# Later gathers for slices 1 to 3, and the last dense layer in four column parts side by side

## The chip, the cores and the metric

One core of a Trainium2 chip runs the whole program. The metric is the device time of one execution in microseconds (us), the median of several runs. Engines: PE (matmul; PEld is its weight load), DVE (vector), ACT (scalar), POOL (GpSimd, which issues the gathers) and SP (which issues plain DMAs).

## The reference

A recommendation tower. For each of 1024 samples, 32 ids pick rows of 64 floats from 32 tables; every pair of the 32 rows is combined through its own 64 x 64 matrix, and the 496 results with 16 dense inputs pass through three layers.

```python
e = jnp.stack([tbl_0[ids[:, 0]], ..., tbl_31[ids[:, 31]]], axis=1)      # 1024 x 32 x 64
z = jnp.einsum('bpe,fpe,bpf->bp', e[:, iu], kernel, e[:, ju])           # 1024 x 496
h = jnp.concatenate([z, dense_ctx], axis=1)                             # 1024 x 512
h = jnp.maximum(h @ W_top1 + b_top1, 0.0)                               # 512
h = jnp.maximum(h @ W_top2 + b_top2, 0.0)                               # 256
y = h @ W_top3                                                          # 1
```

## The kernel before

The batch is cut into 8 slices of 128 samples (t = 0 to 7; TILES in the code), and two slices make a quarter of 256 samples, on which the dense layers run. The 32 fields of a slice are 16 packs of two. Each field is one gather: an indirect DMA that POOL issues (line 356), 128 rows of 64 floats into the ring `raw`, 256 gathers in all, in the order of slices and fields. When both gathers of a pack have landed (`gathered`), PE transposes it (line 611, into `prep_ps`) and ACT copies it to `xt` (line 394, a "fill").

The pair work of a slice is 32 units (NU), of three kinds: F (PE line 570, DVE multiply line 476), C (PE line 600, DVE line 498) and B (PE line 587, DVE lines 517 and 533). A unit's matmuls go to one of three slots of `t_ps`; PE counts `t_done` up by one when they are done, DVE waits for it and multiplies, and PE may use the slot again after that (`prod_done`). The F products are summed on PE in rounds of four units (line 642, into `z_ps`): matmuls with 32 columns of weights, 256 columns each, that rotate over four blocks of 32 result rows. The C and B products are summed along their 64 elements by ACT (line 418, one instruction a cell) and DVE (line 504), those of the last slice by POOL (line 374).

The matrices (`kmat`, 8.29 MB) are loaded by SP in the order in which the first slice needs them. In slices 0 to 3 the units are sorted by the last pack that they need, so that a slice can begin before all its fields are there.

PE, ACT and DVE each follow one list written ahead of time, SCHEDULE: units in order, with fills, rounds of sums and pieces of the dense layers inserted at set unit numbers (`fills_of`, GROUPS_AT, PAIRS_AT). The fills of slices 1 to 3 stand at these places, counted from the slice's own first unit: slice 1 at -5, -2, 1, 4, 8, 13, 17; slice 2 at -6, -2, 1, 4, 8, 12, 20; slice 3 (four packs each) at -6, -3, 4, 10. Slice 4's stand at -19, -12, -4, 4, and slices 5 to 7 have theirs at -20, -12, -4, 4.

POOL has no list of its own. `gather_after(t, field)` is the number of finished units (`t_done`) for which a gather waits: none for the first 16 gathers of slice 0, then (field - 12) // 2, and for later slices (t - 1) * 32 + field, so that a slice's gathers run one unit apart during the slice before it. Gathers whose number is reached already follow one another without a wait. The ring `raw` holds three slices, and from slice 3 on the first gather of each group of eight also waits until the group that was there is used up.

The dense layers of the first three quarters are pieces of PE's list: each result goes to `prep_ps` and is copied by ACT. The last quarter's stand at the end in `t_ps`. The last layer (line 710) takes two matmuls of 256 columns, `w3` one column of weights; ACT copies the row of 256 results (line 441) and issues the store (line 446).

The semaphores named in the text: `t_done` (PE to DVE and POOL), `prod_done` (DVE to PE and ACT), `prep_done` (PE to ACT) and `prep_copied` (ACT to PE).

Of the kernel before, what the change touches and what calls it, by code (L numbers as in the profile page):

```python
# [5 lines left out]
H1, H2 = 512, 256  # L6
P = 128
# [3 lines left out]
QB = 2 * P  # L11
# [24 lines left out]


def gather_after(t, field):


    return (t - 1) * NU + field if t else (field - 12) // 2 if field >= 16 else 0

# [147 lines left out]
TURN_LAG, PIECE_LAG, PIECE_STEP = 16, 24, 8  # L190
SUMS_LAG = 5
LAYER1, LAYER2 = H1 // P, H2 // P
PIECES = LAYER1 + LAYER2 + 1
# [74 lines left out]
def build(nc, ids, tables, kmat, dense, w1, b1, w2, b2, w3, sel, ident, y):  # L268
# [3 lines left out]
    with ctx:  # L272
# [10 lines left out]
        w2_sb = sb("w2_sb", [P, H1 // P, H2])  # L283
        w3_sb = sb("w3_sb", [P, H2 // P])
        b1_sb = sb("b1_sb", [P, H1 // P])
# [10 lines left out]
        h2 = sb("h2", [P, H2 // P, QB])  # L296
        y_sb = sb("y_sb", [1, 2, QB])

# [79 lines left out]
        def _(act):  # L378
# [42 lines left out]
            def copy_layer(q, piece):  # L421
# [9 lines left out]
                if piece < LAYER1:  # L431
                    nc.scalar.activation(h1[:, piece, :], source, ACT.Relu,
                                         bias=b1_sb[:, piece:piece + 1]).then_inc(copied, 1)
                elif piece < LAYER1 + LAYER2:
                    m = piece - LAYER1
                    nc.scalar.activation(h2[:, m, :], source, ACT.Relu, bias=b2_sb[:, m:m + 1]).then_inc(copied, 1)
                else:
                    if q >= 2:

                        act.wait_ge(y_stored[q % 2], 16 * (q // 2))  # L440
                    nc.scalar.activation(y_sb[:, q % 2, :], source[0:1, :], ACT.Copy).then_inc(copied, 1)
                    if q < QUARTERS - 1:
                        act.wait_ge(prep_copied, PREP_COUNT["piece", q, piece])
                    else:
                        act.wait_ge(layer_copied, PIECES)
                    act.dma_start(y[:, q * QB:(q + 1) * QB], y_sb[:, q % 2, :]).then_inc(y_stored[q % 2], 16)

# [101 lines left out]
        def _(pe):  # L549
# [146 lines left out]
            def later_layer(q, piece, out, copied, done):  # L696
# [9 lines left out]
                else:  # L706
                    for t in range(LAYER2):
                        if copied:
                            pe.wait_ge(copied, LAYER1 + t + 1)
                        last = nc.tensor.matmul(out[0:1, :], w3_sb[:, t:t + 1], h2[:, t, :],  # L710
                                                start=(t == 0), stop=(t == LAYER2 - 1))
                last.then_inc(done, 1)
# [87 lines left out]
```

## Time and profile before

| | us |
|---|---|
| median of 3 runs | 483.64 |
| lowest and highest of them | 479.96 and 483.74 |
| the profiled execution, its own time | 483.11 |
| its span, first to last instruction | 481.3 |
| PE busy | 411.4 (85%) |
| DVE busy | 342.4 (71%) |
| ACT busy | 325.4 (68%) |
| POOL busy | 268.3 (56%) |
| mean granted clock of PE | 0.957 of full speed |

The span is what the trace shows; the execution's own time has 1.8 us around it. Each fp32 matmul of the program stands in the trace as two weight loads and two matmuls. "x16" after an instruction is the number of records that were merged into the row. What stands behind "<-" in brackets is what ended the idle time before the instruction; "issue" means that the profile shows nothing that it waited for, "remote" and "another core or an unknown queue" that the signal has no visible sender.

### The profile page before, as it was taken

How to read it: one execution, taken by the hardware profiler on the slowest of the kernel's cores; microseconds unless marked ns; L12 is line 12 of the kernel's file. 1: busy time of each engine (PE TensorE's matmuls, PEld its weight loads, DVE VectorE, ACT ScalarE, POOL GpSimd, SP SyncE). 2: the span in 40 equal slices, each digit the busy share in tenths (PEclk: the TensorE clock that was granted, in tenths of full speed). 3: DMA queues.
4: the chain of work that ended last, by engine and by line, in shares of the span. 5: the costliest groups of instructions: out<-in, count | busy, mean ns of one | idle time of the engine just before them, and what ended most of it. 6: DMA issues, size and time to landing. Idle time of an engine off the chain costs nothing.

```text
span 481.3 us, 12047 instructions
## 1 busy us (share of the span) xinstructions
PE 411.4 (85%) x4144; PEld 280.4 (58%) x4144; DVE 342.4 (71%) x428; ACT 325.4 (68%) x2456; POOL 268.3 (56%) x308
## 2 busy tenths in 40 slices
PE   0554358888898988999999999999999999999997
PEld 0332245655556555767666666666666566666875
DVE  0044158889798878788778887888888788877820
ACT  1244215078967887689857897878786978988512
POOL 5757735566556555555545555556555555577400
PEclk9976568999998999999999999999999999999999
DMA  8751101015111111111111111111111111000000
GB/s 278 268 215 27 26 14 24 18 24 155 21 23 21 20 24 21 21 22 22 23 19 20 23 23 21 20 24 21 20 24 23 22 21 20 16 1 3 1 2 0
DMA packets 12756, 19.17 MB, mean 40 GB/s; under 512 B 6036, under 2 KB 6296, under 8 KB 12568
## 3 DMA queue, kind: packets, MB, share of 16 engines
q0 software_dynamic: 8192, 8.40, 9.4%
q1 hardware_dynamic: 2592, 8.29, 4.8%
q10 hardware_dynamic: 1912, 1.71, 1.2%
q8 instruction: 33, 0.54, 0.5%
q14 instruction: 27, 0.22, 0.1%
HBM read 18.39 MB, written 0.00 MB: 38 GB/s over the span
## 4 chain that ended last, share of the span: by engine, by line
PE 74%; DVE 12%; issue 9%; another core or an unknown queue 2%; DMA 2%; POOL 1%; ACT 1%; DVEq 0%
PE t_ps L570 25%; PE z_ps L642 14%; PE t_ps L600 12%; PE t_ps L587 9%; DVE prod L476 6%; PE prep_ps L657 5%; PE prep_ps L611 3%; DVE prod_a L498 2%; PE prep_ps L704 2%; DVE prod_a L517 2%; PE t_ps L657 2%; DVE zb L504 1%; DMA raw<-tbl,ids_sb 1%; POOL raw L356 1%
## 5 line engine op out<-in xcount | busy, mean ns | idle before, releaser
L356 POOL DMA_INDIRECT raw<-tbl,ids_sb x256 | 242.3, 946 | 172.5 <-issue 48.0
L418 ACT ACTIVATE prod_a<-prod_a 128x64 f32<-128x64 f32 x1184 | 283.9, 243 | 69.0 <-DVE prod_a L533 33.5
L418 ACT ACTIVATION_READ_ACCUMULATOR prod_a<-prod_a 128x1 f32 x1184 | 223.9, 189 | 7.5 <-issue 7.5
L476 DVE TENSOR_TENSOR prod<-t_ps,xt 128x1024 f32<-128x1024 f32 x128 | 155.7, 1220 | 63.6 <-PE t_ps L570 25.5
L570 PEld LDWEIGHTS t_ps<-xt,k_sb 64*128 64x128 f32 x2048 | 136.5, 193 | 55.3 <-issue 31.7
L570 PE MATMUL t_ps<-xt,k_sb 64*128 64x128 f32 x2048 | 151.7, 286 | 19.3 <-issue 10.1
L498 DVE TENSOR_TENSOR prod_a<-t_ps,raw 128x1024 f32<-128x1024 f32 x64 | 78.0, 1219 | 23.6 <-PE t_ps L600 14.7
L600 PE MATMUL t_ps<-k_sb,xt 64*128 64x512 f32 x256 | 74.7, 654 | 19.3 <-issue 14.1
L517 DVE TENSOR_TENSOR prod_a<-t_ps,raw 128x768 f32<-128x768 f32 (+2 forms) x96 | 62.9, 683 | 31.1 <-PE t_ps L587 24.0
L642 PE MATMUL z_ps<-prod,sel_sb 128*32 128x256 f32 x1024 | 71.7, 390 | 4.0 <-issue 3.7
L587 PE MATMUL t_ps<-k_sb,xt 64*128 64x384 f32 (+5 forms) x448 | 66.0, 402 | 3.5 <-issue 1.8
L642 PEld LDWEIGHTS z_ps<-prod,sel_sb 128*32 128x32 f32 x1024 | 33.9, 111 | 39.0 <-issue 22.6
L587 PEld LDWEIGHTS t_ps<-k_sb,xt 64*128 64x128 f32 x448 | 43.0, 191 | 21.9 <-issue 9.6
L394 ACT ACTIVATE xt<-prep_ps 128x512 f32<-128x512 f32 (+2 forms) x47 | 21.0, 446 | 42.6 <-PE prep_ps L611 31.0
L504 DVE TENSOR_REDUCE zb<-prod_a 128x8 f32<-128x512 f32 x76 | 49.7, 676 | 0.0
L611 PE MATMUL prep_ps<-ident_sb,raw 128*128 128x128 f32 x128 | 26.4, 305 | 20.8 <-DMA raw<-tbl,ids_sb 15.1
L600 PEld LDWEIGHTS t_ps<-k_sb,xt 64*128 64x128 f32 x256 | 21.0, 191 | 32.5 <-issue 23.7
L611 PEld LDWEIGHTS prep_ps<-ident_sb,raw 128*128 128x128 f32 x128 | 14.3, 144 | 38.0 <-issue 25.8
L374 POOL TENSOR_TENSOR prod_a<-prod_a 128x512 f32<-128x512 f32 (+4 forms) x40 | 24.3, 607 | 9.7 <-DVE prod_a L498 7.2
L533 DVE TENSOR_TENSOR prod_a<-t_ps,raw 128x128 f32<-128x128 f32 x64 | 18.0, 281 | 0.0
L657 PE MATMUL prep_ps<-zbt,w_sb 128*128 128x256 f32 x48 | 13.6, 405 | 0.0
L657 PE MATMUL prep_ps<-zt,w_sb 128*128 128x256 f32 x48 | 12.3, 379 | 0.0
(30 smaller groups left out, 91.1 us busy)
## 6 DMA issues: line engine op xcount, KB each, us to landing
raw<-tbl,ids_sb POOLq DMA_INDIRECT x256
k_sb<-kmat SPq DMA_DIRECT2D x4, 768.0 KB
k_sb<-kmat SPq DMA_DIRECT2D x4, 512.0 KB
k_sb<-kmat SPq DMA_DIRECT2D x4, 448.0 KB, 4.6
k_sb<-kmat SPq DMA_DIRECT2D x4, 256.0 KB
w_sb<-w ACTq DMA_DIRECT2D x1, 1024.0 KB
w_sb<-w ACTq DMA_DIRECT2D x1, 512.0 KB
ids_sb<-ids SPq DMA_DIRECT2D x1, 128.0 KB, 2.4
```

What stands on the lines that cost most here:

```text
L356: nc.gpsimd.indirect_dma_start(raw[:, n % RING, begin:begin + EMBED], None, tables[2 * k + f], bass.IndirectOffsetOnAxis(ap=ids_sb[:, t, 2 ...
L418: last = nc.scalar.activation(product, product, ACT.Copy, accum_out=zb[:, unit[1], at:at + 1])
L476: nc.vector.tensor_tensor(prod[:, own].rearrange("p n (m b) -> p (n m) b", b=P), t_ps[:, slot].rearrange("p n (m b) -> p (n m) b", b=P), x ...
L498: nc.vector.tensor_tensor(out, product, rows.unsqueeze(1).broadcast_to([P, 2, W]), ALU.mult).then_inc(prod_done, 1)
L504: nc.vector.tensor_reduce(zb[:, unit[1], begin + n * cells:begin + (n + 1) * cells], prod_a[:, NTH[unit] % ARING, n, 0:cells * EMBED].rear ...
L517: return nc.vector.tensor_tensor(out[:, :, cols], product[:, :, cols], rows[:, fields * EMBED:(fields + cells) * EMBED].unsqueeze(1).broad ...
L570: last = nc.tensor.matmul(t_ps[:, slot, n, i * P:(i + 1) * P], k_sb[rows, cols], xt[rows, x, :], start=True, stop=True)
L587: last = nc.tensor.matmul(product[:, n, cell * EMBED:(cell + cells) * EMBED], xt[rows, slot_of(t, GROUP * g + field // 2), :], k_sb[rows, ...
L600: last = nc.tensor.matmul(product[:, n, :], xt[rows, slot_of(t, k), :], k_sb[rows, COL["C", k, j]], start=True, stop=True)
L611: last = nc.tensor.transpose(prep_ps[:, n * P:(n + 1) * P], raw[:, group % RING, at * P:(at + 1) * P], ident_sb[:])
L642: last = nc.tensor.matmul(z_ps[32 * group:32 * group + 32, 0:ZBLOCKS * P], sel_sb[:, 30 - 2 * pos:62 - 2 * pos], prod[:, (t * NF + u) % FR ...
L657: return nc.tensor.matmul(out, w1_sb[:, part, m * P:(m + 1) * P], z, start=(part == ZBLOCKS), stop=(part == ZBLOCKS - 1 and half != 0))
```

## The change

Two edits. First, the gathers of slices 1, 2 and 3 wait for 10, 8 and 4 more finished units than before; those of slice 0 and of slices 4 to 7 keep their numbers. Second, the last dense layer is cut into four parts of 64 columns. `w3` gets 32 columns of weights, of which only the first is not zero; part n writes result rows 32n to 32n+31 and columns 0 to 63, so the four parts lie side by side on different rows. ACT copies 128 x 64 instead of 1 x 256, and the store takes every 32nd row, four rows of 256 B. The host reads `y` as 16 rows of 64 and reshapes it.

```diff
+GATHER_LATER = {1: 10, 2: 8, 3: 4}
 def gather_after(t, field):
-    return (t - 1) * NU + field if t else (field - 12) // 2 if field >= 16 else 0
+    return (t - 1) * NU + field + GATHER_LATER.get(t, 0) if t else (field - 12) // 2 if field >= 16 else 0
...
+YPARTS = 4
+YROWS, YCOLS = P // YPARTS, QB // YPARTS
...
-        w3_sb = sb("w3_sb", [P, H2 // P])
+        w3_sb = sb("w3_sb", [P, H2 // P, YROWS])
-        y_sb = sb("y_sb", [1, 2, QB])
+        y_sb = sb("y_sb", [P, 2, YCOLS])
...
-                    nc.scalar.activation(y_sb[:, q % 2, :], source[0:1, :], ACT.Copy).then_inc(copied, 1)
+                    nc.scalar.activation(y_sb[:, q % 2, :], source[:, 0:YCOLS], ACT.Copy).then_inc(copied, 1)
-                    act.dma_start(y[:, q * QB:(q + 1) * QB], y_sb[:, q % 2, :]).then_inc(y_stored[q % 2], 16)
+                    act.dma_start(y[q * YPARTS:(q + 1) * YPARTS, :], y_sb[0:P:YROWS, q % 2, :]).then_inc(y_stored[q % 2], 16)
...
-                        last = nc.tensor.matmul(out[0:1, :], w3_sb[:, t:t + 1], h2[:, t, :],
-                                                start=(t == 0), stop=(t == LAYER2 - 1))
+                        for part in range(YPARTS):
+                            last = nc.tensor.matmul(out[part * YROWS:(part + 1) * YROWS, 0:YCOLS], w3_sb[:, t, :],
+                                                    h2[:, t, part * YCOLS:(part + 1) * YCOLS],
+                                                    start=(t == 0), stop=(t == LAYER2 - 1))
...
+    w3_rows = np.zeros((P, H2 // P, YROWS), w1.dtype)
+    w3_rows[:, :, 0] = np.asarray(W_top3).reshape(-1, P).T
```

On POOL the gathers keep their order; what a row shows beside them is on which semaphores they wait. The program's start on POOL before, gathers of slice 0 (32), then of later slices:

```order
L356 DMA raw<-tbl,ids_sb 128x64 [waits ids_in]
L356 DMA raw<-tbl,ids_sb 128x64 x15
L356 DMA raw<-tbl,ids_sb 128x64 [waits t_done] x16
L356 DMA raw<-tbl,ids_sb 128x64
L356 DMA raw<-tbl,ids_sb 128x64 [waits t_done] x63
L356 DMA raw<-tbl,ids_sb 128x64 [waits t_done,prod_done]
L356 DMA raw<-tbl,ids_sb 128x64 [waits t_done] x7
```

The same place on POOL now:

```order
L362 DMA raw<-tbl,ids_sb 128x64 [waits ids_in]
L362 DMA raw<-tbl,ids_sb 128x64 x15
L362 DMA raw<-tbl,ids_sb 128x64 [waits t_done] x80
L362 DMA raw<-tbl,ids_sb 128x64 [waits t_done,prod_done]
L362 DMA raw<-tbl,ids_sb 128x64 [waits t_done] x7
```

Slice 1's first gather had no wait and has one now; the numbers waited for, which the rows don't show, are 10, 8 or 4 higher for the 96 gathers of slices 1 to 3.

On PE the rows are the same but for the last layer's. The program's end on PE before (`h` is h1 or h2):

```order
L657 MATMUL t_ps<-zt,w_sb 128x128 x2
L642 MATMUL z_ps<-prod,sel_sb 32x256 x16
L657 MATMUL t_ps<-zt,w_sb 128x128 x8
L704 MATMUL t_ps<-h,w_sb 128x256 x8
L710 MATMUL t_ps<-h,w_sb 1x256 x2
```

The program's end on PE now:

```order
L663 MATMUL t_ps<-zt,w_sb 128x128 x2
L648 MATMUL z_ps<-prod,sel_sb 32x256 x16
L663 MATMUL t_ps<-zt,w_sb 128x128 x8
L710 MATMUL t_ps<-h,w_sb 128x256 x8
L717 MATMUL t_ps<-h,w_sb 32x64 x8
```

Two matmuls of 1 x 256 have become eight of 32 x 64; nothing around them moved. The same holds for the three earlier places of that layer.

## Rows read from the trace of the kernel before

**Rows 1.** The page: the span, and its 40 equal slices of PE.

```profile
span 481.3 us, 12047 instructions
...
PE   0554358888898988999999999999999999999997
...
PEclk9976568999998999999999999999999999999999
```

**Rows 2.** Chain that ended last, 0 to 66 us: start us, us, what.

```profile
21.31 4.65 another core or an unknown queue
...
30.07 4.70 another core or an unknown queue
...
44.61 11.02 issue
...
60.13 4.97 issue
```

**Rows 3.** Timeline of POOL, 0 to 95 us: start, us, instruction, idle before.

```profile
3.38 1.09 POOL L356 DMA_INDIRECT raw<-tbl,ids_sb  x1 [2.93 <-DMA ids_sb<-ids]
...
22.30 0.94 POOL L356 DMA_INDIRECT raw<-tbl,ids_sb  x1 [0.30 <-issue]
26.18 0.95 POOL L356 DMA_INDIRECT raw<-tbl,ids_sb  x1 [2.94 <-remote]
...
32.44 0.95 POOL L356 DMA_INDIRECT raw<-tbl,ids_sb  x1 [0.30 <-issue]
35.03 0.95 POOL L356 DMA_INDIRECT raw<-tbl,ids_sb  x1 [1.64 <-remote]
...
46.28 0.95 POOL L356 DMA_INDIRECT raw<-tbl,ids_sb  x1 [0.30 <-issue]
...
60.04 0.94 POOL L356 DMA_INDIRECT raw<-tbl,ids_sb  x1 [0.30 <-issue]
64.93 0.95 POOL L356 DMA_INDIRECT raw<-tbl,ids_sb  x1 [3.94 <-remote]
```

**Rows 4.** Timeline of PE, 0 to 95 us.

```profile
10.53 0.45 PE L611 MATMUL prep_ps<-ident_sb,raw 128*128 128x128 f32 x1 [10.53 <-DMA raw<-tbl,ids_sb]
...
42.75 1.86 PE L570 MATMUL t_ps<-xt,k_sb 64*128 64x128 f32 x16
55.64 2.08 PE L600 MATMUL t_ps<-k_sb,xt 64*128 64x512 f32 x4 [11.02 <-issue]
...
58.05 2.08 PE L570 MATMUL t_ps<-xt,k_sb 64*128 64x128 f32 x16
65.11 2.08 PE L570 MATMUL t_ps<-xt,k_sb 64*128 64x128 f32 x16 [4.97 <-issue]
...
89.59 1.16 PE L570 MATMUL t_ps<-xt,k_sb 64*128 64x128 f32 x16 [0.59 <-DVE prod L476]
90.69 1.93 PE L642 MATMUL z_ps<-prod,sel_sb 128*32 128x256 f32 x32
```

**Rows 5.** Timeline of DVE, 0 to 95 us.

```profile
58.38 1.22 DVE L476 TENSOR_TENSOR prod<-t_ps,xt 128x1024 f32<-128x1024 f32 x1 [14.70 <-PE t_ps L600]
```

**Rows 6.** Timeline of ACT, 0 to 75 us.

```profile
19.79 0.24 ACT L418 ACTIVATE prod_a<-prod_a 128x64 f32<-128x64 f32 x1
...
49.44 0.26 ACT L394 ACTIVATE xt<-prep_ps 128x128 f32<-128x128 f32 x1
...
64.73 0.28 ACT L394 ACTIVATE xt<-prep_ps 128x128 f32<-128x128 f32 x1 [0.57 <-remote]
```

**Rows 7.** Busy time by stretch: stretch, us, PE, PEld, DVE, ACT, POOL, clock, DMA.

```profile
65.10:90.70 25.60, 22.76 (x246) 16.09 (x246) 21.64 (x27) 7.95 (x61) 14.13 (x16) 0.87 0.11 20
```

**Rows 8.** Timeline of PE, its weight loads and ACT, the last layer.

```profile
478.04 1.23 PE L710 MATMUL t_ps<-h,w_sb 128*1 128x256 f32 x4
...
478.67 0.09 PEld L710 LDWEIGHTS t_ps<-h,w_sb 128*1 128x1 f32 x2 [0.55 <-ACT h L436]
479.31 0.37 ACT L441 ACTIVATE y_sb<-t_ps 1x256 f32<-1x256 f32 x1 [0.68 <-PE t_ps L710]
```

More of the change, by code:

```diff
@@ L785 @@
         "b2": np.ascontiguousarray(np.asarray(b_top2).reshape(-1, P).T),
-        "w3": np.ascontiguousarray(np.asarray(W_top3).reshape(-1, P).T),
+        "w3": w3_rows,
         "sel": sel,
@@ L795 @@
            for n, a in arrays.items()}
-    y = nc.dram_tensor("y", (1, BATCH), mybir.dt.float32, kind="ExternalOutput").ap()
+    y = nc.dram_tensor("y", (QUARTERS * YPARTS, YCOLS), mybir.dt.float32, kind="ExternalOutput").ap()
     build(nc, tables=[aps.pop(f"tbl_{f}") for f in range(FIELDS)], y=y, **aps)
```

## The prediction

> **What bounds the kernel now.** I read the page first: the span of 481.3 us and the slices [rows 1]. The span is cut into 40 slices of 12 us: PE is 80% or more busy from the seventh on, but only 30 to 59% from the second to the sixth, and the granted clock sinks to 0.5 in the fifth. So something is wrong between about 20 and 70 us, in the first slice of the batch; after it PE works at a steady pace to the end, and what is saved there should move the whole rest forward. Next the chain that ended last [rows 2]: in the first 66 us four pieces stand out, two of "another core or an unknown queue" (4.65 and 4.70 us) and two of "issue" (11.02 and 4.97 us), 25.3 us in which the engine on the path waits for nothing that the profile can name. Gathers explain none of it: the first transpose ran at 10.53 on rows whose gathers began at 3.38, so a gather lands within 7.2 us even beside the load of kmat [rows 3, 4].
>
> What the engines did in those stretches is the key. PE finished the tenth unit (line 570) at 44.61; DVE's multiply of it starts at 58.38, 13.8 us later, and that start is put down to PE [rows 4, 5]. ACT's copy of the next pack ended at 49.70, and PE's unit that needs it starts at 55.64. ACT itself makes two copies at 49.44 and 64.73 with only seven sums of line 418 between them; at 0.24 us a sum [rows 6] that is 1.7 us of work in 15 us. So hand-overs between engines arrive late, and ACT's own instructions crawl, all at once. I call this a freeze.
>
> POOL's rows show when [rows 3]. Its gathers stand 1.25 us apart where nothing gates them: 16 from 3.38 to 22.30, 6 from 26.18 to 32.44, and 21 from 35.03 to 60.04. Each of these runs has one freeze in its later part, and each freeze ends shortly after the run: the last gathers end at 23.24, 33.39 and 60.98, and the engines are released at 25.96, 34.77 and 64.73 [rows 2, 3, 6]. The lags are 2.7, 1.4 and 3.8 us, growing with 16, 6 and 21 gathers. Once the gathers are gated one to a unit (from 64.93 on), "issue" and "another core" pieces of that size are gone from the chain. My reading: a long unbroken run of gathers holds up the other engines' signals and instructions, and a pause of POOL lets them go. A DVE and a POOL that stop because they need the held-up signal would look alike, so this is an inference; the lengths (a 22 us freeze under a run of 21, short ones under short runs) speak for it.
>
> **The gathers of slices 1 to 3.** Nothing is removed or added on POOL: the same 256 gathers stand in the same order, now 240 with a wait on PE's count of finished units. The first slice's 32 keep their conditions, so all up to the one issued at 46.28 stays as it was, the freeze that begins near 42 included. What changes is the next: the second slice's gather f ran after f units, so its first eleven followed without a break up to 60.04 [rows 3]; now gather f waits for 10+f units. After 46.28 POOL stops until unit 10 is signalled, and the later ones come one to a unit, at 1.7 us or so a unit (15 units, the 13th to the 27th, in the 25.6 us of [rows 7]), slower than POOL's 1.25. The run of 21 becomes a run of 10.
>
> The sum, against the profiled execution's 483.11 us:
> 1. End of the freeze: last gather ends 46.28 + 0.95 = 47.2, plus a lag for a run of ten. Between 1.4 us (6 gathers) and 2.7 (16), I take 1.9: release at 49.1. ACT's copy needs 0.3 more: unit 11 starts at 49.4 instead of 55.64.
> 2. From there before: 2.08 us for unit 11, 0.4 for a transpose, 2.08 for unit 12, to 60.13, then 4.97 us of waiting for ACT's copy at 64.73 [rows 2, 4, 6]. The copy has 1.7 us of sums ahead of it, so with no freeze it is there before unit 12 ends. Unit 13 starts at 49.4 + 4.5 = 53.9 instead of 65.11: 11.2 us saved. Bounds: with the lag of 3.8 us 9.3, with 1.4 us 11.7.
> 3. Catching up: from 65.1 to 90.7 PE was 22.76 us busy and DVE 21.64 of 25.6, at a clock of 0.87 [rows 7]. PE began it cold: the same 16 records took 2.08 us at 65.11 and 1.16 at 89.59 [rows 4]. Without the long stop it has less to make up. What can go is between 0 and 2.8 us (25.6 less PE's 22.8); nothing favours an end, I take 1.4, the middle.
> 4. Cost of the later gathers: a slice's groups are transposed 7 to 15 units after the last gather that they need may start. Seven units at 1.7 us are 11.9 us, against at most 7.2 us to land [rows 3, 4]. Nothing waits: 0. If that cover were gone, each late fill would cost PE what it is late. Slices four to seven already live with 5 to 6 units and show no such wait in the chain. Queued behind POOL's new waits are only more gathers and, at the very end, its sums of the last slice, whose gates don't move.
> 5. The ends of slices 2 and 3 overlap with the next slice's start (slice 3's first four may go with slice 2's last, slice 4's with slice 3's), which makes two runs of five. The nearest row is the run of 6 with its 4.70 us piece in the chain [rows 2, 3]; that ran beside the kmat load, and the gated runs (up to four in a row) cost nothing seen. Between 0 and 2 x 4.7 us; I take 0, nearest to the gated runs.
>
> **The last layer.** Two matmuls of 256 columns with one column of weights become eight of 64 columns with 32 columns of weights, four side by side in different row blocks of the result. PE records two per fp32 matmul, so 4 records become 16. Before: 1.23 us at the end of the program, including 0.55 for ACT's h2 [rows 8]; only the second half, 478.67 to 479.27, 0.6 us, is after that wait. After, that half is 8 records. By the feature sums, which have the same 32 columns and rotate over four blocks, 32 records take 1.93 us, 0.06 each; by the transform of 128 columns 16 take 1.16, 0.07 each [rows 4]. So 8 records take 0.5 to 0.6 us: gain 0 to 0.1, and if all four parts truly cost a quarter, 0.45. In the middle the same layer stands three times on PE's path: by the same rows 0.9 to 1.2 us for 16 records against about 1.03; 0. ACT's copy handles 64 instead of 256 columns: 0.37 us falls to about 0.24, the 64-column sum's time [rows 6, 8]. The store is four rows of 256 B instead of one of 1 KB, issued the same way: 0, with 0.2 us either way. Altogether 0.2 us saved, between -0.2 and 0.8.
>
> The Trainium skill (TensorEngine Tiling (Array Packing), Instruction Overhead) speaks against this half: each matmul carries about 60 cycles whatever its columns, and one should not take the tiling from a dimension that is small already. By it four parts of 64 columns would gain little over one of 256. The trace's 0.06 us a record agrees that the issue, not the columns, sets the time of such short pieces; the sum would not change by it.
>
> Total: 11.2 + 1.4 + 0 + 0.2 = 12.8 us, so 483.1 - 12.8 = 470.3 us. The profiled execution lies 0.5 us under the median of the three runs (483.64), well inside what can be told; a measurement of this kernel tells about 1%, 4.8 us, from no change.
>
> **Rivals.**
> A. The freeze is not the gathers' doing. Then something else held ACT and the signals from 42 to 64.7, it stays, and the first slice is as slow: about 483 us, the last layer's 0.2 aside. For it: while frozen, POOL alone ran on undisturbed at 1.25 us, and the runs also end because POOL needs a signal. Against: three freezes, three runs, none in the gated rest. The Trainium skill (SBUF — State Buffer, SBUF: two separate sides) supports this rival: ports of engines and of DMAs cannot contend, and PE, ACT and DVE's own pair never wait on anyone, so gathers could not slow ACT. The trace shows ACT at 15 us for 1.7 us of work beside them, which that rule leaves unexplained. Chance 10%.
> B. The gathers do it, but short runs too: the runs of five set off freezes of up to 4.7 us each, or the one at 42 outlasts the pause. 470.3 + 2.4 to 9.4: around 475 us. Chance 13%.
> C. Slower: a run of five at a slice's end sets off a freeze as long as the long one, 44.6 to 64.7, 20 us, since PE then has a gather's gate to feed and POOL a backlog to work off. It decides if five in a row are enough to start what lasts on its own. 470.3 + 20 = 490 us. Against: POOL must stop there as soon as units stop. Chance 4%.
> Forecast: 73%.
>
> **Numbers.** The forecast's own bounds: 9.3 + 0 - 0.2 = 9.1 saved gives 474.0; 11.7 + 2.8 + 0.8 = 15.3 gives 467.8. Leaving out A and C and the far end of B (14 to 18%) the range reaches to 479, and I open the low side to 466.5, as the break may also shorten the freeze before 47. Faster by over 1% (under 478.8): the forecast, most of B, rounded with doubts about the reading, 0.86; within 1%: A and the rest of B, 0.10; slower 0.04.
>
> **What would show it.** After: POOL's gathers pause at 47.2 for about two microseconds; PE's unit 11 starts near 49.4 and unit 13 near 54, and the chain's 11.02 and 4.97 us pieces shrink to a few us in all; DVE sees unit 10 near 49; no transpose waits on a gather after the first slice; the two runs of five pass with no piece over 1 us; the first slice ends 11 to 14 us earlier and every later one takes what it took. It is wrong if PE still stands until 64 with POOL silent (A), if new "issue" pieces stand at the ends of slices 2 and 3 (B, C), or if a gather is waited for (step 4). The last dense layer at the program's end should show 16 records within 1.3 us, and ACT's copy of it about 0.24.

## The result, and the profile after

The change makes the kernel slightly slower. After: median 486.43 us of 8 runs (484.63 to 487.5); before, beside it on the same chip: 482.15 us of 8 (479.96 to 483.74). The ratio is 1.0094, with an interval of 1.0071 to 1.0117. The forecast was 470.3 us, at the latest 479.

The kernel before takes about 420 us in some comparisons and 481 to 490 us in others, on the same chip even, so every experiment below is read only against the kernel before that ran beside it. I write "at 420" and "at 481 to 490" for these two levels. The result above, and the profile that the prediction read, are at 481.

The page of the changed kernel, its span and PE's 40 slices (12.1 us each), beside [rows 1]:

```profile
span 485.7 us, 12143 instructions
...
PE   0664989879889599989999899999999999999997
...
PEclk9995789998999699978999999999999999999999
```

The hole from the second to the sixth slice has become smaller: the fifth and sixth digit were 3 and 5 and are 9 and 8. New are the 5 in the 14th slice (158 to 170 us) and the clock's 6 and 7 in the 14th and the 18th (206 to 219 us). The execution of this profile took 487.5 us.

The first slice went as forecast. The chain that ended last, 0 to 66 us (start us, us, what), beside [rows 2]:

```profile
29.91 4.68 another core or an unknown queue
...
44.65 4.82 issue
```

The 11.02 us piece is 4.82 us now, and the 4.97 us piece behind it is gone. POOL's timeline (start us, us, instruction, idle before), 41 to 79 us, beside [rows 3]:

```profile
46.08 0.94 POOL L362 DMA_INDIRECT raw<-tbl,ids_sb  x1 [0.30 <-issue]
49.35 0.94 POOL L362 DMA_INDIRECT raw<-tbl,ids_sb  x1 [2.32 <-remote]
51.82 0.94 POOL L362 DMA_INDIRECT raw<-tbl,ids_sb  x1 [1.53 <-PE t_ps L606]
...
78.57 0.94 POOL L362 DMA_INDIRECT raw<-tbl,ids_sb  x1 [0.30 <-issue]
```

The run of gathers ends at 46.08 + 0.94 = 47.02 and POOL stands for 2.32 us, as said. The row at 78.57 is the 49th gather of the program; keep it in mind. PE, 41 to 68 us, beside [rows 4]:

```profile
42.57 2.08 PE L576 MATMUL t_ps<-xt,k_sb 64*128 64x128 f32 x16
49.47 2.08 PE L606 MATMUL t_ps<-k_sb,xt 64*128 64x512 f32 x4 [4.82 <-issue]
51.47 0.48 PE L617 MATMUL prep_ps<-ident_sb,raw 128*128 128x128 f32 x1
51.88 3.74 PE L576 MATMUL t_ps<-xt,k_sb 64*128 64x128 f32 x32
55.55 1.94 PE L648 MATMUL z_ps<-prod,sel_sb 128*32 128x256 f32 x32
```

Unit 11 starts at 49.47 (before 55.64) and units 12 and 13 stand in one row without a gap, so unit 13 starts at about 53.8 (before 65.11). ACT and DVE at the release, all engines' timeline, beside [rows 5, 6]:

```profile
48.30 0.26 ACT L424 ACTIVATE prod_a<-prod_a 128x64 f32<-128x64 f32 x1 [0.50 <-issue]
49.00 0.20 ACT L424 ACTIVATION_READ_ACCUMULATOR prod_a<-prod_a 128x1 f32 x1 [0.44 <-issue]
49.11 0.26 ACT L400 ACTIVATE xt<-prep_ps 128x128 f32<-128x128 f32 x1
49.11 1.23 DVE L482 TENSOR_TENSOR prod<-t_ps,xt 128x1024 f32<-128x1024 f32 x1 [5.62 <-remote]
49.27 0.25 ACT L424 ACTIVATE prod_a<-prod_a 128x64 f32<-128x64 f32 x1
```

Until 49.0 ACT puts 0.7 us between two starts, while the instructions themselves take as long as ever (0.26 us inside, 0.25 outside); from 49.11 on its instructions follow one another at once, and DVE gets unit 10's signal at the same moment.

Then the gain is lost. A table of when chosen rounds of the feature sums (line 648, [rows 4] has the third at 90.69) begin on PE, from the two timelines; a round is four F units, and 32 of them make the program:

| round | before us | after us | difference |
|---|---|---|---|
| 1st | 67.11 | 55.55 | -11.6 |
| 4th, slice 0 done | 104.29 | 92.00 | -12.3 |
| 6th | 132.08 | 123.66 | -8.4 |
| 8th | 154.72 | 145.79 | -8.9 |
| 9th | 173.79 | 170.97 | -2.8 |
| 12th | 210.29 | 207.15 | -3.1 |
| 13th | 226.61 | 230.60 | +4.0 |
| 14th | 239.81 | 245.19 | +5.4 |
| 28th | 421.16 | 426.10 | +4.9 |

Three losses, 3.9, 6.1 and 8.5 us (to the 14th round), lie at the ends of slices 1, 2 and 3 of the gathers; together with small drift 17.7 us, against 12.3 won. After the 14th round the two kernels run in step. The first goes with a run of six gathers from 101.54 us; no single stop in it is over 1.9 us. The second, in POOL's timeline from 154 to 165 us:

```profile
154.31 0.94 POOL L362 DMA_INDIRECT raw<-tbl,ids_sb  x1 [1.05 <-PE t_ps L576]
155.56 0.94 POOL L362 DMA_INDIRECT raw<-tbl,ids_sb  x1 [0.31 <-DVE prod_a L539]
...
161.81 0.94 POOL L362 DMA_INDIRECT raw<-tbl,ids_sb  x1 [0.30 <-issue]
164.60 0.94 POOL L362 DMA_INDIRECT raw<-tbl,ids_sb  x1 [1.85 <-remote]
```

DVE's timeline of the same stretch:

```profile
157.22 1.23 DVE L504 TENSOR_TENSOR prod_a<-t_ps,raw 128x1024 f32<-128x1024 f32 x1 [0.70 <-PE t_ps L576]
164.36 1.22 DVE L482 TENSOR_TENSOR prod<-t_ps,xt 128x1024 f32<-128x1024 f32 x1 [5.92 <-remote]
```

And the chain that ended last:

```profile
158.44 5.89 another core or an unknown queue
```

Seven gathers in a row, DVE without its signal from 158.44 to 164.36, and the release 1.6 us after the run's end at 162.75: the picture of the first freeze, small. The third loss, PE between 210 and 217 us, beside a run of seven gathers from 206.50 to 213.99:

```profile
210.75 0.31 PE L593 MATMUL t_ps<-k_sb,xt 64*128 64x64 f32 x1 [0.19 <-issue]
211.45 0.21 PE L593 MATMUL t_ps<-k_sb,xt 64*128 64x64 f32 x1 [0.39 <-issue]
212.17 0.75 PE L593 MATMUL t_ps<-k_sb,xt 64*128 64x192 f32 x2 [0.51 <-issue]
```

Here PE itself crawls, its records starting some 0.7 us apart, where at 58.67 us fourteen of the same line took 1.79 us together, and its clock, 0.80 in 206 to 231 us, makes the work behind it slow too.

The stretch that answers to [rows 7] (from unit 13 to the third round; columns as there):

```profile
53.80:78.70 24.90, 22.06 (x246) 15.75 (x245) 20.90 (x26) 8.06 (x61) 13.34 (x15) 0.90 0.10 19
```

24.9 us instead of 25.6. The last layer at the end of the program, PE, its weight loads and ACT, beside [rows 8]:

```profile
482.36 0.32 PE L717 MATMUL t_ps<-h,w_sb 128*32 128x64 f32 x8
...
483.00 0.32 PE L717 MATMUL t_ps<-h,w_sb 128*32 128x64 f32 x8 [0.32 <-ACT h L442]
483.38 0.22 ACT L447 ACTIVATE y_sb<-t_ps 128x64 f32<-128x64 f32 x1 [0.44 <-PE t_ps L717]
```

Sixteen records from 482.36 to 483.32, 0.96 us; the half behind ACT's wait takes 0.32 us where it took 0.6, and ACT's copy 0.22.

### The profile page after: what moved, and what is told of

The parts are those of the page before. It is cut to its first block, busy times and chain, and to the rows that moved or that the text cites. A ratio compares the mean times of both kernels' runs of the same rounds, so it can differ in the third digit from the quotient of the medians.

```text
span 485.7 us, 12143 instructions
## 1 busy us (share of the span) xinstructions
PE 420.9 (87%) x4192; PEld 288.1 (59%) x4192; DVE 342.4 (71%) x428; ACT 325.2 (67%) x2456; POOL 267.6 (55%) x308
## 4 chain that ended last, share of the span: by engine, by line
PE 73%; DVE 12%; issue 7%; POOL 3%; another core or an unknown queue 2%; DMA 2%; ACT 1%; ACTq 0%; DVEq 0%
PE t_ps L576 24%; PE z_ps L648 14%; PE t_ps L606 12%; PE t_ps L593 9%; DVE prod L482 6%; PE prep_ps L663 5%; DVE prod_a L504 3%; POOL raw L362 3%; PE prep_ps L617 2%; PE prep_ps L710 2%; PE t_ps L663 2%; DMA raw<-tbl,ids_sb 1%; DVE prod_a L523 1%; DVE zb L510 1%
## 5 line engine op out<-in xcount | busy, mean ns | idle before, releaser
L576 PE MATMUL t_ps<-xt,k_sb 64*128 64x128 f32 x2048 | 158.0, 291 | 20.7 <-DVE prod L482 10.5
L576 PEld LDWEIGHTS t_ps<-xt,k_sb 64*128 64x128 f32 x2048 | 140.3, 197 | 57.1 <-issue 33.3
L606 PE MATMUL t_ps<-k_sb,xt 64*128 64x512 f32 x256 | 75.1, 656 | 12.5 <-issue 7.1
L593 PE MATMUL t_ps<-k_sb,xt 64*128 64x384 f32 (+5 forms) x448 | 72.2, 413 | 5.3 <-issue 3.4
L593 PEld LDWEIGHTS t_ps<-k_sb,xt 64*128 64x128 f32 x448 | 45.1, 196 | 26.2 <-issue 14.7
L617 PE MATMUL prep_ps<-ident_sb,raw 128*128 128x128 f32 x128 | 26.6, 307 | 19.4 <-DMA raw<-tbl,ids_sb 17.2
L606 PEld LDWEIGHTS t_ps<-k_sb,xt 64*128 64x128 f32 x256 | 21.3, 193 | 25.4 <-issue 16.2
L415 ACT ACTIVATE zt<-z_ps 128x256 f32<-128x256 f32 x8 | 3.0, 374 | 16.7 <-PE z_ps L648 8.5
```

Source lines behind the costliest of these rows:

```text
L576: last = nc.tensor.matmul(t_ps[:, slot, n, i * P:(i + 1) * P], k_sb[rows, cols], xt[rows, x, :], start=True, stop=True)
L593: last = nc.tensor.matmul(product[:, n, cell * EMBED:(cell + cells) * EMBED], xt[rows, slot_of(t, GROUP * g + field // 2), :], k_sb[rows, ...
L606: last = nc.tensor.matmul(product[:, n, :], xt[rows, slot_of(t, k), :], k_sb[rows, COL["C", k, j]], start=True, stop=True)
L617: last = nc.tensor.transpose(prep_ps[:, n * P:(n + 1) * P], raw[:, group % RING, at * P:(at + 1) * P], ident_sb[:])
```

## The experiments

"Ratio" is the kernel against the kernel before beside it, with the interval in brackets.

**The pace of the gathers spread, and the last layer alone.** The theory: the runs at the slices' ends are the trouble. In the first kernel (e1, cut from the changed kernel) the ten gathers of extra distance are given back one at a time over slices 1 to 3; in the second (e3), the gathers are as before and only the last layer is changed. The two edits in that order, e3's behind the expectations:

```diff
 def gather_after(t, field):
-    return (t - 1) * NU + field + GATHER_LATER.get(t, 0) if t else (field - 12) // 2 if field >= 16 else 0
+    if t == 0:
+        return (field - 12) // 2 if field >= 16 else 0
+    n = (t - 1) * FIELDS + field
+    return n + max(0, -(-LATER * (SPREAD - n) // SPREAD))    # LATER, SPREAD = 10, 96
```

> The changed kernel, but the ten units of delay of slice 1's first gather are given back one at a time over the 96 gathers of slices 1 to 3 instead of at their two or three ends. Theory 1 (a run of six or more gathers in a row stops the hand-overs between engines; the changed kernel wins 12 us in slice 0 and loses 17 in three such runs of 6, 7 and 7 gathers at about 102, 154 and 207 us): the 12 us stay and the 17 are gone, so the last round of feature sums starts about 12 us earlier than in the kernel before and the time is 468 to 472 us. Rival (the loss comes from gathers that are later at all, so that PE, DVE or ACT meet them at a worse moment): the loss stays for the most part, 480 to 487 us.

> The kernel before with the last dense layer in four column parts alone, all gathers as before. Forecast of the prediction: 0.2 us saved, between -0.2 and 0.8; 482 us. If the layer's 24 extra instructions a time on PE had part in the loss, it would be 1 us or more slower.

```diff
-GATHER_LATER = {1: 10, 2: 8, 3: 4}
+GATHER_LATER = {}
```

Measured: spread 421.64 us, ratio 1.0023 (1.0006 to 1.0041); layer only 420.69, ratio 1.0002 (0.9987 to 1.0016). The kernel before beside them took 420.44. So the last layer is worth nothing that can be measured, as forecast. The spread could not be judged: the freeze that it was to avoid was absent from the kernel before too. The layer-only profile, whose gathers are those of before, shows how the same program looks at 420. POOL's first, 17th and 35th gather:

```profile
3.39 1.09 POOL L362 DMA_INDIRECT raw<-tbl,ids_sb  x1 [2.94 <-DMA ids_sb<-ids]
...
23.50 0.94 POOL L362 DMA_INDIRECT raw<-tbl,ids_sb  x1 [0.30 <-issue]
...
45.97 0.94 POOL L362 DMA_INDIRECT raw<-tbl,ids_sb  x1 [0.30 <-PE t_ps L576]
```

and PE's first round of sums:

```profile
42.35 1.93 PE L648 MATMUL z_ps<-prod,sel_sb 128*32 128x256 f32 x32
```

126 gathers follow one another 1.25 us apart with no break, to 159.58, and nobody is stopped: the first round begins at 42.35 us, where it began at 67.11 in the profile that the prediction read. A long run of gathers is therefore not enough for a freeze. Another mark tells the levels apart over the whole program: PE's idle time with nothing seen to wait for ("issue") is 31.6 us in the kernel before at 481 and none here, and DVE's idle time before a signal with no visible sender ("remote") is 20.6 us there and none here.

**Landing waits in the changed kernel, and bursts.** Two more of the same comparison. In e2 POOL waits in slices 1 to 4, at every second pack, until the gather that it has just issued has landed, so that no run is longer than four; in e4 (on the kernel before) the gathers of slices 4 to 7 go in runs of eight, all when the last of the eight was due.

```diff
+                    if f == 1 and k % 2 == 1 and 1 <= t <= 4:
+                        pool.wait_ge(gathered[n % RING * GROUP + at], 32 * (n // RING + 1))
```

```diff
+    if t >= 4 and field % 8 >= 8 - BURST_OF:    # BURST_OF = 8
+        field |= 7
```

> The changed kernel with its own delays of 10, 8 and 4 units, but in slices 1 to 4 POOL waits after every fourth gather until that gather has landed, a pause of 1 to 1.5 us. The gathers are then as late as in the changed kernel or later. Theory 1: no run is longer than four, the three losses at the slices' ends vanish, 468 to 473 us. Rival (late gathers): 486 us or more.

> The kernel before, but in slices 4 to 7 each group of eight gathers waits for the number that its last gather had, so that they go as 16 runs of eight. No gather's latest start moves, only the first seven of each group are held back. Theory 1: each run of eight costs as the runs of 7 at 154 and 207 us did, 6 to 7 us, so up to 16 x 6.5 = about 100 us slower. Rival (runs don't matter, only late gathers or the start of the program): within 3 us of the kernel before.

Measured, at 420: e2 458.11 us, 1.0904 (1.0868 to 1.0939), and e4 536.18 us, 1.2753 (1.2706 to 1.2799). Neither says anything of a freeze. The groups of PE's instructions (busy us, mean ns, idle before and its releasers) show the cause in e2:

```profile
L619 PE MATMUL prep_ps<-ident_sb,raw 128*128 128x128 f32 x128 | 30.8, 319 | 41.2 <-DMA raw<-tbl,ids_sb 40.8 <-ACT xt L402 0.2
```

PE waits 40.8 us for gathers that have not landed, and 87.4 us in e4; 15.8 us of it stands in the layer-only kernel too. My sizing was at fault: with the lead of 5 units eight gathers of 1.25 us, which need 10 us, cannot be there in time when they are issued late. A gather that comes too late is waited for, and that is its own, much larger price.

**The change itself at 420, early runs, and fewer extra waits.** e5 is the changed kernel unaltered. e6 issues the gathers of slices 2 to 7 in runs of eight when the first of the eight was due, so that none is later than before. e7 puts the landing waits into the kernel before, in slice 1 and the second half of slice 0. e8 is e1 again.

```diff
+EARLY_RUN = 8
 ...
+    if t >= 2:
+        field -= field % EARLY_RUN
```

```diff
+                    if f == 1 and k % 2 == 1 and (t == 1 or t == 0 and k >= PACKS // 2):
+                        pool.wait_ge(gathered[n % RING * GROUP + at], 32 * (n // RING + 1))
```

> The changed kernel once more, beside a kernel before that may run at about 420 us (as in the first four experiments) or at about 482 us (as in the first comparison). Theory 1 (hand-overs stop under runs of gathers, but only where the kernel before takes 482 us): at 420 us there is nothing to win or lose, PE's rounds of sums come at the times of the kernel before to within 1 us and the ratio is 0.998 to 1.005; at 482 us the ratio is 1.009 again. Rival (the changed order costs 4 us of its own, through later gathers): 4 us slower at 420 us too, ratio 1.01.

> The kernel before, but in slices 2 to 7 each group of eight gathers waits only for the number of its first one, so that they go as 24 runs of eight, early rather than late: no gather can be missed by a transpose. Only the length of the runs differs. Theory 1: where the kernel before takes 482 us, each run of eight stops the hand-overs for 5 to 7 us, 60 to 150 us slower in all; where it takes 420 us nothing happens (the first 126 gathers ran there in one piece without a stop), within 1%. Rival (runs are harmless everywhere): within 1% at either.

> The kernel before, but POOL waits for the landing of every fourth gather in the second half of slice 0 and in slice 1, so that no run there is longer than four. Theory 1: where the kernel before takes 482 us, the stops at 30 and 42 to 65 us go, 10 to 16 us faster (466 to 472); where it takes 420 us, 0 to 3 us slower for the later gathers. Rival: no gain at 482 us.

> The same kernel as in the first experiment. At 420 us: ratio 1.002 as there. At 482 us, theory 1: 468 to 472 us, the 12 us of slice 0 won and the three losses at the slices' ends gone; rival (later gathers cost as such): 480 or more.

Measured, beside a before of 420.88 us on another chip: the changed kernel 421.79, ratio 1.002 (1.0005 to 1.0035); early runs 421.19, 0.9999 (0.9981 to 1.0017); landing waits 436.25, 1.0361 (1.0334 to 1.0387), where I had expected 0 to 3 us, PE waiting 31.4 us for gathers instead of 15.8; the spread 421.55, 1.0013 (0.9995 to 1.0031). At this level 24 runs of eight gathers cost nothing, and the change costs 0.9 us; the rival of e5, 4 us at this level too, falls.

**The same early runs and the spread at 490.** e9 is e6 and e10 is e1 again; this time the kernel before took 489.69 us.

> The kernel with early runs of eight gathers once more, on whatever chip comes. If the kernel before runs at about 482 us there, theory 1 expects 60 to 150 us more (24 runs of eight, 5 to 7 us each where PE has no slack), the rival within 1%. If it runs at about 420 us, both expect no difference, and the run only adds one more chip to the count of those without stops.

> The kernel whose delay is given back one unit at a time, on the same chip. If the kernel before runs at about 482 us: theory 1 expects 468 to 472 us, the rival 480 or more. If at 420 us: ratio 1.000 to 1.003.

Measured: early runs 618.16 us, ratio 1.2627 (1.2558 to 1.2696); spread 492.62, ratio 1.0049 (1.001 to 1.0088). This separates the theories on runs: the same program that loses nothing at 420 loses 128 us here, 5.35 us for each of its 24 runs of eight. PE beside such a run (POOL's gathers from 197 to 205.96):

```profile
204.18 1.95 PE L575 MATMUL t_ps<-xt,k_sb 64*128 64x128 f32 x14 [2.13 <-DVE prod L481]
207.17 0.37 PE L575 MATMUL t_ps<-xt,k_sb 64*128 64x128 f32 x1 [1.05 <-issue]
207.90 2.81 PE L575 MATMUL t_ps<-xt,k_sb 64*128 64x128 f32 x17 [0.36 <-issue]
```

But the spread kernel lost its gain too, as its rival expected, and it has no run of more than four gathers after 59 us. Its rounds stand at -10.8 us (3rd), -6.8 (5th), -2.0 (8th), +1.4 (10th), +6.6 (13th), +8.3 (15th) against before: a steady leak in place of three steps. These differences are taken against the one trace of the kernel before, of 483.11 us; the kernel before beside e10 took 6.6 us more and left no trace, so up to 6.6 us of the later ones need not be e10's own. (The first four rounds of e9, whose gathers are those of before up to there, lie within 0.3 us of that trace.) Even so some 12 us of leak are left. Long runs are one way to lose the time; they are not the whole of it.

**The whole distance kept, and runs cut to four.** e11 keeps the ten units of distance in all later slices, so that no gather has to be made up anywhere; for this the fills of slices 3 to 7 had to move later. e12 is e7 again.

```diff
-GATHER_LATER = {1: 10, 2: 8, 3: 4}
+GATHER_LATER = {1: 10, 2: 10, 3: 10, 4: 10, 5: 10, 6: 10, 7: 8}
-GROUPS_AT = {3: (-6, -3, 4, 10), 4: (-19, -12, -4, 4)}
+GROUPS_AT = {3: (-6, -3, 4, 13), **{t: (-8, -2, 4, 13) for t in (4, 5, 6)}, 7: (-10, -3, 3, 12)}
```

> The changed kernel, but the gathers of all later slices wait for ten more units (eight in the last slice), and the fills of slices 4 to 7 stand later in the list to match, so that slices never have to give the delay back and there is one gather to a unit throughout. Theory 2 (where the kernel before takes 482 to 490 us, the other engines lose time once gathers follow one another faster than about one in 1.4 us, a long run costs much, a faster average some; the changed kernel and the spread one both lose what they won because slices 1 to 3 must take 10 more gathers in the same units): the 12 us of slice 0 stay, ratio 0.970 to 0.980 there. Rival (later gathers cost by being later): ratio 1.00 or more there. Where the kernel before takes 420 us: 0.998 to 1.005 by both, unless a transpose meets a gather that has not landed.

> The kernel before with a wait for every fourth gather's landing in the second half of slice 0 and in slice 1, as in the seventh experiment, where it cost 15 us at 420 us. At 482 to 490 us, theory 2: the stop from 42 to 65 us goes, but slice 1's gathers come late (a pause makes 1.6 us a gather), so 0 to 12 us won over the kernel before, and PE's unit 13 starts before 57 us. Rival (the stops have another cause): unit 13 starts at 65 us and the 15 us are lost on top. At 420 us: 1.036 as before.

Measured, beside a before of 480.95 us (on the chip that had shown 420.88): e11 496.75, 1.0328 (1.029 to 1.0367); e12 486.99, 1.0134 (1.0106 to 1.0163). Both total times miss what theory 2 expected, and both hide what matters. In e11 the rounds stand at -12.3 us (4th), -12.5 (6th), -12.8 (9th), -12.7 (13th) and -12.6 (15th): the 12 us of the first slice are kept whole through the stretch in which the changed kernel lost 17.7 (13th round at 213.87 us, before 226.61, after 230.60). Then they go, from the first fill of slice 4 on, for the most part for a reason of my own making, the fills that I had moved:

```profile
249.97 0.65 PE L617 MATMUL prep_ps<-ident_sb,raw 128*128 128x128 f32 x4
254.55 2.08 PE L606 MATMUL t_ps<-k_sb,xt 64*128 64x512 f32 x4 [3.93 <-ACT xt L400]
```

ACT's copy comes after a queue of sums, and PE waits 3.93 us for it here, and again at 314, 372, 429 and 445 us (slices 5 to 7), 16.5 us in all, where before and after have no such wait. From the 15th round to the 29th e11 loses 26.7 us, so some 10 us of it have other causes. Through slice 3 the gain stayed with the distance; that it would stay to the end if no fill came late is not shown.

In e12 the freeze of 42 to 65 us is gone altogether, with runs of four from 35 us on: the first round is at 44.66 us, 22.5 us before its old place. At 108.29 us the landing waits end, POOL's gates are long passed, and it issues 20 gathers in a row. DVE beside them:

```profile
111.22 1.22 DVE L500 TENSOR_TENSOR prod_a<-t_ps,raw 128x1024 f32<-128x1024 f32 x1
121.09 1.22 DVE L478 TENSOR_TENSOR prod<-t_ps,xt 128x1024 f32<-128x1024 f32 x1 [8.65 <-remote]
```

DVE stands 8.65 us, later 5.25 and 7.35 us more, and the 6th round is at +0.2 us, the 7th at +5.5. The first two of these stops end inside the run of gathers, which goes on to 132.96 us; only the last ends after it. That is the same pattern, produced at will in another place: take the run out of slice 0, and the freeze appears where the gathers are made up.

**Landing waits in slices 1 to 3, a slower pace, early runs of four; at 420.** e13 carries the landing waits to slice 3. e14 puts a 128 x 256 fill of scratch memory on POOL behind each gather from the 17th to the 128th, which makes the pitch 1.44 us. e15 is e6 with runs of four.

The condition of e13's wait against e7's, and e14's fill:

```diff
-(t == 1 or t == 0 and k >= PACKS // 2)
+(1 <= t <= 3 or t == 0 and k >= PACKS // 2)
```

```diff
+                    if p >= PACKS // 2 and p < 4 * PACKS:
+                        if p > PACKS // 2 or f:
+                            pool.wait_ge(filled, 2 * (p - PACKS // 2) + f)
+                        nc.gpsimd.memset(filler[:], 0.0).then_inc(filled, 1)
```

> The kernel before with the wait for every fourth gather's landing kept on through slices 2 and 3, so that the run of 20 gathers, behind which the twelfth experiment lost its 20 us again between its fourth and fifth round of sums, is cut into fours too. Where the kernel before takes about 482 us: theory 2 (runs of more than four or five do the harm) keeps some 15 to 20 us, 462 to 470 us, unless transposes wait for gathers at 1.6 us each; rival (any early win is given back by the end of slice 1): 482 or more. Where it takes 420 us: 435 to 460 us by both, since PE then outruns gathers of 1.6 us.

> The kernel before, but POOL clears a small scratch tile (256 columns) after each gather from the 17th to the 128th, which sets these gathers 1.5 to 1.7 us apart with no wait for a landing. It tells a run's length from its pace. If what harms is a pace above one gather in about 1.4 us, no stop follows at 482 us even in long runs, and PE's first round of sums comes before 50 us, as in the twelfth experiment (44.7). If the pauses help only because a landed gather clears something, the stop from 42 us on stays. At 420 us: 2 to 20 us slower by both, for gathers that come later.

> The kernel before, but in slices 2 to 7 gathers go in early runs of four (48 of them) instead of eight. At 482 to 490 us theory 2 expects little beyond the kernel before, whose own runs are of 1 to 4: within 10 us, against the 128 us of the runs of eight; if the cost were in proportion to the gathers that stand in runs, it would be about half of the 128 us. At 420 us: within 1%.

Measured, before 420.92 us: e13 457.76, 1.0869 (1.082 to 1.0918); e14 436.80, 1.0358 (1.0334 to 1.0382); e15 420.77, 0.9998 (0.9978 to 1.0018). At this level these brakes on the gathers cost and no run does.

**The same three at 490.** e16, e17 and e18 are e13, e14 and e15 again.

> As the thirteenth experiment, which came in a call where the kernel before takes 421 us. At 482 to 490 us theory 2: 462 to 472 us, 15 to 20 us won and kept; rival: 482 or more. At 421 us: 458 again.

> As the fourteenth experiment; its gathers stood 1.44 us apart in long runs. At 482 to 490 us: if the pace is what harms (above one in about 1.4 us), PE's first round of sums comes before 50 us; if the length of the run is, it comes near 67 us as in the kernel before. At 421 us: 437 again.

> As the fifteenth experiment. At 482 to 490 us: within 10 us of the kernel before if a run of four is nearly free, some 60 us more if the cost goes by the gathers that stand in runs. At 421 us: within 1%.

Measured, before 490.25 us: e16 493.38, 1.0093 (1.005 to 1.0136); e17 488.23, 0.9956 (0.9921 to 0.9992); e18 524.56, 1.0747 (1.0664 to 1.083). The 48 runs of four cost 34 us, 0.7 us each: not nothing, as I had put it, but about an eighth of what a run of eight costs. e16 was expected at 462 to 472 us and missed that. Against the trace of before at 481, it is 19.4 us ahead at the fourth round, 8.0 at the ninth and 4.1 at the 12th, a leak like e10's (again up to some 7 us of it may be the slower kernel before's), and stands at +6.5 at the 13th: its landing waits end, ten gathers go in a row from 212.5 us, and DVE stands 9.71 us. e17, with the slower pace, is the only kernel that beat before at this level, by less than half a per cent, and it lost 3.6% at 420. Its first round of sums is at 51.55 us instead of 67.11, but the slower pace did not prevent the freeze, it came later, in DVE's timeline:

```profile
53.36 1.22 DVE L486 TENSOR_TENSOR prod<-t_ps,xt 128x1024 f32<-128x1024 f32 x1
67.84 1.22 DVE L486 TENSOR_TENSOR prod<-t_ps,xt 128x1024 f32<-128x1024 f32 x1 [13.27 <-remote]
```

This stop ends while the gathers go on at 1.44 us each, to 72.7 us.

No version was faster than the kernel before at both levels, and none by more than half a per cent at either.

## Why the prediction was wrong

What the runs leave standing is this. At 481 to 490 the units lose time where POOL issues gathers beyond the one to a unit, and the ten gathers that the change takes out of slice 0's run have to be issued somewhere. The distance of gathers ahead of units falls from ten units of delay to none between the ends of slices 1 and 3 (10, 8, 4, 0), so POOL makes up ten gathers there. The price can be read off three kernels, from the best round to the 15th: the changed kernel loses 12.3 + 5.4 = 17.7 us for ten, 1.8 each; e11, which makes up none there, loses none. The spread kernel loses between 10.8 + 8.3 = 19.1 and, less the 6.6 us by which the kernel before beside it was slower, 12.5 us, 1.3 to 1.9 each. The first two together show that it is the making up and not the delay that costs, the third that it costs also where the ten come singly; how much less, if any, can't be told. In sum, 12.3 us won and 17.7 lost leave the changed kernel 5.4 us behind at the 15th round, 4.9 at the 28th and 4.4 at the end (spans of 485.7 and 481.3). That bunching costs even with nothing to make up, e9 and e18 show.

The timeline of the 256 gathers fits this from the other side. The 49th gather starts at 73.67 us before and at 78.57 after, the last at 414.28 and 419.21, and the spans are 481.3 and 485.7. POOL's timeline of before:

```profile
73.67 0.95 POOL L356 DMA_INDIRECT raw<-tbl,ids_sb  x1 [0.30 <-issue]
...
414.28 0.95 POOL L356 DMA_INDIRECT raw<-tbl,ids_sb  x1 [0.30 <-issue]
```

and the last gather of after (its 49th stands above, at 78.57):

```profile
419.21 0.94 POOL L362 DMA_INDIRECT raw<-tbl,ids_sb  x1 [0.31 <-issue]
```

The gathers were never caught up: 4.9 us late at the 49th, 4.9 us late at the last, 1.0 to 5.9 in between. Between them a gather takes on average (414.28 - 73.67) / 207 = 1.65 us in both, and 1.4 us at 420 (63.4 to 352.3 in the layer-only run). That the stream of gathers sets the pace of the whole kernel at 481 fits all of this; it is argued and not shown, since gathers wait for units and units for gathers, and in other kernels (the spread one, 4.9 us late at the 49th and 11.2 at the last) the lateness still grows.

Point by point:

- "End of the freeze: release at 49.1", unit 11 at 49.4: 49.11 and 49.47. The lag behind the last gather, taken at 1.9, was 2.1. Right.
- "Unit 13 starts at 53.9 instead of 65.11": about 53.8. Right.
- Catching up 1.4: the stretch is 24.9 us instead of 25.6, 0.7, and the fourth round is 12.3 us earlier in all, against 12.6. Right, the middle slightly high.
- These steps are right at this level only: at 420 there is no freeze to end, and the change gains nothing (e5). That the result came at the level of the profile was luck, and the prediction did not know that there are two.
- Step 4, "Nothing waits: 0". No transpose waits on a gather after the first slice, as said, so the cover held. But it asked only whether a gather comes late for its reader, and not what the making up costs the others. That term was missing, and it is the size of the whole gain.
- **The step that failed is the fifth**: "Between 0 and 2 x 4.7 us; I take 0, nearest to the gated runs." It measured 17.7 us, nearly twice the step's own upper end of 9.4, which the forecast's own bounds (9.1 to 15.3 us saved) had left to rival B. Three ends of slices, not two, cost, as slice 1's end has its two gathers as well. The runs that formed were of 6, 7 and 7 gathers and not of five: each begins right after POOL has waited 1.05 to 1.11 us for a unit, and while it goes on the units that the next gathers wait for are finished too. The nearest row was indeed the run of 6 with its 4.70 us piece, between the prices of four and eight (0.7 and 5.35 us a run, e18 and e9), and I chose the other neighbour. For that neighbour the reading itself was wrong: the gated runs of four did not "cost nothing seen". POOL's run of four that begins at 314.30 us in the kernel before ends at 319.00, and PE stops in the middle of a unit from 319.04 on, in PE's timeline:

```profile
319.97 0.84 PE L570 MATMUL t_ps<-xt,k_sb 64*128 64x128 f32 x10 [0.93 <-issue]
```

  The same stop of 0.92 to 0.95 us follows the ends of the runs of four at 266.75, 345.33 and 371.77 us; the layer-only kernel at 420 has none.
- Behind it stood a sentence of the first part: "what is saved there should move the whole rest forward". It did not move forward: from slice 4 on the gathers are at the same distance from the units as before, and the gain was gone when that distance was reached.
- Rival A falls: the freeze of slice 0 ended with the shorter run, and with runs of four it did not come there (e12). The rule of the Trainium skill beside it (SBUF — State Buffer, SBUF: two separate sides), that such traffic cannot slow ACT at its ports, leaves unexplained the crawl at 0.7 us a start; the trace does not contradict it, as ACT's instructions keep their length (0.26 us) and only their starts stand apart. But half of its doubt was sound: the gathers alone are not enough, as the 126 in a row at 420 show.
- Rivals B and C named the right places. B's price, 2.4 to 9.4 us, was too small; C's, one freeze of 20, was near in sum and wrong in form: three losses of 3.9, 6.1 and 8.5 us. C's argument against, "POOL must stop there as soon as units stop", holds only when its gates are not passed already. I gave C 4%; the measured case lies between the two prices, where no rival stood.
- The last layer: 0.2 us forecast; its halves are 0.3 us shorter and the copy 0.15, and the run with it alone measures 1.0002. Right within what can be told. With what the Trainium skill says (TensorEngine Tiling (Array Packing), Instruction Overhead), that each matmul has a fixed cost whatever its columns, the run agrees in the sum, as the parts gained nothing that can be measured; the measured 0.32 us for eight records, 0.04 each, is less than the 0.06 that I had taken.

What stays open: what makes the level 420 or 481 to 490 (not the chip alone: one chip showed both), and by which resource the gathers hold the others. It is not that the gathers themselves are slow: by the packets of the trace, the gathers 23 to 43 of the kernel before, those of the freeze, have their last packet done 2.0 to 2.4 us after POOL begins the issue, as at 420 (median 2.1). A distance of ten units throughout, with fills placed so that ACT can keep up, would be the version to try next; it was not tried.

## What to carry to other kernels

When a stall is removed at the start of a pipelined kernel, ask what each producer has to make up before the state is the same as before, and price that; a delay that is given back later is not a delay removed. Where the delay was kept, as in e11 through slice 3, the gain was kept with it; whether it can be kept to the end was not shown. And read a profile's large stall together with how the kernel runs when the stall is absent: had a profile at 420 been at hand, it would have shown that the run of gathers alone does nothing. Look also for the small form of a large stall before you call a neighbouring row free.

## What the runs showed of the hardware

- Gathers issued back to back on POOL (0.944 us busy, 1.25 us pitch, 128 rows of 256 B each) can hold up other engines at 481 to 490: DVE's signals arrive 5 to 14 us late, and ACT starts instructions 0.7, 1.4 or 2.1 us apart (before, 43 to 65 us) while each takes its usual time. The release often comes 1.4 to 3.8 us after the last gather of the run; some stops end inside the run (e12 at 121.09, e17 at 67.84 us).
- The cost goes up steeply with the length of a run at 490: 0.7 us for a run of four (e18), 5.35 for a run of eight (e9); both nothing at 420 (e15, e6).
- A slightly slower pitch is no cure: at 1.44 us the freeze still came, 13.27 us long (e17).
- The same program has two levels, 420 and 481 to 490 us. At the first, the layer-only kernel has no freeze, PE 93% busy (389.3 of 419.1 us) and 126 gathers in one run; at the second, the kernel before has 85% and a freeze of 22 us. Which of them a comparison meets is not fixed by the kernel or the chip (one chip gave 420.88 and 480.95 us).
